# Output stage joined to the mixing stage, nine sums kept in SBUF, and token tiles of four neighbouring tokens a partition

## The reference

```python
proj = xn @ in_proj_w + in_proj_b            # 256 -> 768
v = proj[..., :256]
for i in range(2):                           # two orders
    ctrl = proj[..., (i + 1) * 256:(i + 2) * 256]
    h = implicit_filter(...)                 # one causal filter per channel, 2048 taps
    v = fft_conv(v, h)                       # causal convolution along the tokens
    xc = depthwise_conv3(ctrl) + conv_b
    v = v * xc * sigmoid(xc @ gate_w + gate_b)
mixed = v @ out_proj_w + out_proj_b
h = bitlinear(xn, w_fc) + gate * (xn @ v_ffn.T @ fast_b.T @ u.T)
ffn = bitlinear(relu(h) ** 2, w_proj)        # 256 -> 1024 -> 256, ternary weights
out = x + mixed + ffn
```

## Time and profile before

| | |
|---|---|
| median of 3 runs | 948.92 us (948.15 to 949.27) |
| the profiled execution | 947.57 us |
| its span, first to last instruction | 946.0 us |
| TensorE busy with matmuls | 842.4 us (89%) |
| TensorE busy with weight loads | 699.2 us (74%) |
| VectorE, ScalarE, GpSimd busy | 633.3, 496.6, 248.4 us |
| DMA | 151.4 MB, 160 GB/s over the span |
| mean granted TensorE clock | 0.959 |

### The profile page before, as it was taken

One profiled execution on the slowest core, in us unless ns is written; L12 is line 12 of the kernel. 1 busy time (PEld: TensorE's weight loads), 2 busy tenths in 40 slices (PEclk: granted clock), 3 DMA queues, 4 the chain that ended last, 5 costly groups with the idle time before them and its releaser, 6 DMA issues.

```text
span 946.0 us, 26422 instructions
## 1 busy us (share of the span) xinstructions
PE 842.4 (89%) x9894; PEld 699.2 (74%) x9895; DVE 633.3 (67%) x1041; ACT 496.6 (52%) x694; POOL 248.4 (26%) x267
## 2 busy tenths in 40 slices
PE   3937999999999964999999999979999999984995
PEld 1325878888888853888888888868888888873885
DVE  6953898998989973456565565556556656653885
ACT  6422877777777772344444444434445344434761
POOL 1023555646646501011121121211112111110111
PEclk9977999999999986899999999999999999995999
DMA  6363224233242138587778868766887777696897
GB/s 182 115 192 134 91 92 177 89 130 136 89 155 111 78 104 261 91 177 175 164 151 195 183 156 176 144 162 153 179 162 173 184 164 168 125 195 148 250 320 273
DMA packets 86866, 151.41 MB, mean 160 GB/s; under 512 B 13013, under 2 KB 62566, under 8 KB 85798
## 3 DMA queue, kind: packets, MB, share of 16 engines
q1 hardware_dynamic: 74918, 107.50, 47.6%
q0 software_dynamic: 11472, 41.69, 13.1%
q10 hardware_dynamic: 432, 1.64, 0.5%
HBM read 102.11 MB, written 48.69 MB: 159 GB/s over the span
## 4 chain that ended last, share of the span: by engine, by line
PE 41%; DVE 7%; DMA 6%; issue 5%; ACT 1%; POOL 0%; DVEq 0%; SPq 0%; ACTq 0%; POOLq 0%
PE pp L1112 13%; PE py L1131 12%; PE pf L1084 11%; PE pf L1090 3%; DVE xb L969 2%; DMA out<-GC 2%; PE py L1099 2%; DMA GC<-xf_hbm 2%; DVE r L974 1%; DVE pp L964 1%; DMA xf_hbm<-xb 1%; DVE r_lo L979 1%; DMA lead<-filters 1%; DMA tokens<-xnT_hbm 1%; PE po L415 1%
## 5 line engine op out<-in xcount | busy, mean ns | idle before, releaser
L1131 PEld LDWEIGHTS py<-vwin,lead 64*64 64x64 f32 x5120 | 134.6, 134 | 30.5 <-issue 30.5
L1044 ACT ACTIVATE r_hi<-r 128x512 fp32r<-128x512 f32 x128 | 80.8, 631 | 137.7 <-DVE r L974 137.7
L1131 PE MATMUL py<-vwin,lead 64*64 64x128 f32 (+4 forms) x5120 | 148.3, 267 | 5.2 <-issue 3.1
L1039 ACT ACTIVATE r<-pf,fscale 128x512 f32<-128x512 f32 x128 | 87.9, 687 | 122.5 <-PE pf L1090 120.4
L979 DVE TENSOR_TENSOR r_lo<-r,r_hi 128x512 fp32r<-128x512 f32 x128 | 103.7, 810 | 68.4 <-ACT r_hi L1044 68.4
L1112 PE MATMUL pp<-wproj,r_hi 128*128 128x256 f32 x512 | 135.7, 298 | 9.9 <-DVE r_lo L979 3.6
L1084 PE MATMUL pf<-tokens,split_a 128*128 (+1 forms) x512 | 140.2, 395 | 0.0
L1112 PE MATMUL pp<-wproj,r_lo 128*128 128x256 f32 x512 | 127.2, 282 | 0.0
L1112 PEld LDWEIGHTS pp<-wproj,r_hi 128*128 128x128 f32 x512 | 96.4, 188 | 26.8 <-issue 9.0
L456 POOL TENSOR_SCALAR lead<-lead,norms 128x256 f32<-128x256 f32 x64 | 114.1, 1794 | 3.4 <-POOL norms L450 3.4
L616 DVE SCALAR_TENSOR_TENSOR xc<-ctrl,taps,xc 128x512 f32<-128x512 f32 x128 | 97.2, 778 | 18.8 <-ACT xc L688 18.1
(11 more groups left out here) (164 smaller groups left out, 1546.4 us busy)
## 6 DMA issues: line engine op xcount, KB each, us to landing
lead<-filters SPq DMA_DIRECT2D x128, 320.0 KB, 6.0
xnT_hbm<-split_b SPq DMA_DIRECT2D x32, 512.0 KB, 3.1
tokens<-xnT_hbm POOLq DMA_DIRECT2D x32, 512.0 KB, 7.1
lead<-in_attn_x SPq DMA_DIRECT2D x16, 512.0 KB, 3.8
gc_hbm<-xc SPq DMA_DIRECT2D x16, 512.0 KB, 2.6
xb<-in_attn_x POOLq DMA_DIRECT2D x16, 512.0 KB, 7.5
GC<-gc_hbm SPq DMA_DIRECT2D x32, 256.0 KB, 7.8
GC<-xf_hbm SPq DMA_DIRECT2D x16, 512.0 KB, 7.9
```

The costliest lines, as they stand in the source:

```text
L1039: act.activation(r[j][:, :], pf[j][:, :], ACT.Relu, scale=fscale[:, m:m + 1]).then_inc(relu_done, 1)
L1044: act.activation(r_hi[j][:, :], r[j][:, :], ACT.Copy).then_inc(r_hi_done, 1)
L1131: last = pe.matmul(py[g % 2][q * BW:(q + 1) * BW, side, l, :, A:NB], tile[rows, q * PAIR + l, j * BW:(j + 1) * BW], vwin[g % 2][rows, q, l ...
```

## The change

1. **Joined.** The output stage's work stands in `mix_stage`'s block, with no barrier ahead of it. Its PSUM tiles are the mixing stage's (`pT` on `py`, `po` on `pf` and `pp`), the split `yg` lies where the ternary weights lay, and the output weights are split in the last iteration. The first two chunks' transposes are put before the last two `proj`. The copy to `ys` is gone: TensorE reads `V` itself as the stationary operand of the transposes, whose 128 columns lie 128 values apart there. The loops of the output part are written out.
2. **Nine sums kept.** The sums of chunks 7 to 15 are made and stay in `GC1`, whose first-order gates are used up by then; only chunks 0 to 6 go through `xf_hbm`. The output part begins with the kept chunks (`position`). Seven chunks' gates are loaded during the second order's iterations (`ahead`).
3. **Token tiles.** Tokens `p * 4 + i` stand at partition `p`, so that the four tokens of a partition are neighbours in HBM, for the loads of `x` in this stage and the writes of `out`. The stationary operands of `proj` and `projected` are read by a step of four to match.
4. The first two filter tiles of the mixing stage, not one, are requested at the end of `project_stage`.

```diff
+KEPT = NCH // ORDERS + 1
+FIRST_KEPT = NCH - KEPT
+GATES = NCH - KEPT
...
+        pT = [p[:, :, :, :, :].rearrange("p r l n a -> p (r l n a)").rearrange("p (t k j) -> p t k j", t=TB, k=KT) for p in py]
+        po = [pf[:, :, :].rearrange("p j (t d) -> p (j t) d", d=D), pp[:, :, :]]
+        ygs = [[half_[:, part, :].rearrange("p (k t) -> p k t", k=KT) for part in range(2)] for half_ in splits]
+        out_tiles = out.rearrange("n (q p i) d -> (n q) p i d", i=TT, p=P)
...
+            def ahead(m, g):
+                if m == 0 and g == GPI - 1:
+                    sp.wait_ge(y_out, GROUPS // ORDERS + 2)
+                if m == 2 and g == 0:
+                    sp.wait_ge(xf_saved, 16 * FIRST_KEPT)
+                    load_wo(sp, wo)
+                piece = m * KT + g // KT - 1
+                if g % KT and 0 <= piece < GATES * KT:
+                    load_gates(sp, piece // KT, (piece % KT,))
...
-            x_tiles = x.rearrange("n (q i p) d -> (n q) p i d", i=TT, p=P)
+            x_tiles = x.rearrange("n (q p i) d -> (n q) p i d", i=TT, p=P)
...
+            for p in range(NCH):
+                pool.wait_ge(out_ready, p + 3)
+                pool.dma_start(out_tiles[position(p)], sums[p % KEPT]).then_inc(out_saved[p % KEPT], 16)
...
             for order in range(ORDERS):
-                lagging(dve, order, lambda m, it, first: body(order, m, it, first))
+                lagging(dve, order, lambda m, it, first: body(order, m, it, first), True)
+            gated(0)
             low(NCH - 1, HT - 1)
+            yg_low(0)
+            gated(1)
             scale(NCH - 1)
-            add(NCH - 1)
+            add(NCH - 1, sums[KEPT - 1])
+            yg_low(1)
+            for p in range(2, NCH):
+                gated(p)
+                summed(p - 2)
+                yg_low(p)
+            for p in (NCH - 2, NCH - 1):
+                summed(p)
...
-                        last = pe.matmul(pp[:, i, :], part[m % 2][:, i * P:(i + 1) * P], wproj[:, m, :],
+                        last = pe.matmul(pp[:, i, :], part[m % 2][:, i::TT], wproj[:, m, :],
...
+            def transposed(p):
+                i, c = p % 2, position(p)
+                pe.wait_ge(yg_ready, p + 1)
                 for t in range(TB):
-                    last = pe.transpose(pT[i][:, t, :, :].rearrange("p k j -> p (k j)"), ys[i][:, t, :], ident[:, :])
+                    last = pe.transpose(pT[i][:, t, :, :].rearrange("p k j -> p (k j)"), V[:, :, c // CPB, (c % CPB) * TB + t], ident[:, :])
                 last.then_inc(yT_mm, 1)
...
+            def projected(p):
...
                 for t in range(TT):
-                    ts = slice(t * P, (t + 1) * P)
+                    ts = slice(t, CH, TT)
                     for k in range(KT):
                         last = split_mm(pe, po[i][:, t, :], (ygs[i][0][:, k, ts], ygs[i][1][:, k, ts]),
                                         (wos[0][:, k, :], wos[1][:, k, :]), k == 0, k == KT - 1)
...
+            def stages(far):
+                for order in range(ORDERS):
+                    mixed(order, far)
+                pe.wait_ge(y_out, GROUPS + 2)
+                transposed(0)
+                proj(NCH - 1, HT - 2)
+                transposed(1)
+                proj(NCH - 1, HT - 1)
+                pe.wait_ge(wo_split, 1)
+                pe.wait_ge(relu_done, NCH * HT + 2)
+                projected(0)
+                pe.wait_ge(xf_ready, NCH + 1)
+                for p in range(2, NCH):
+                    transposed(p)
+                    projected(p - 1)
+                projected(NCH - 1)
```

More of the change, by code:

```diff
@@ L896, in body @@
                             sp.sem_inc(mid_loaded[g % 2], 16 * SIDES)
+                        if order:
+                            ahead(m, g)
                         if far:
+                            if first and g == 0:
+                                sp.wait_ge(T_loaded[1], 16 * SIDES)
                             wait_alone(sp, group_mm, G + 2, sp_passed)
@@ L901, in body @@
                                 wait_alone(sp, far_used, G * FARS + (j + 1), sp_passed)
[L902 to L912 removed]
+                if order == 0:
+                    lagging(sp, order, body)
+                    return
@@ new lines, in loads @@
+                for m in range(ITERS):
+                    body(m, m + ITERS, False)
+            def ahead(m, g):
[7 more added lines that the diff above has]
+                    load_gates(sp, piece // KT, (piece % KT,))
@@ new lines, in gates @@
+            def gates(p):
+                wait_alone(sp, yg_ready, p - GATES + 3, sp_passed)
+                load_gates(sp, p)
+            def stages(far):
+                for order in range(ORDERS):
+                    loads(order, far)
+                for p in range(GATES, NCH):
+                    gates(p)
+                    if p >= KEPT:
+                        wait_alone(sp, out_saved[p - KEPT], 16, sp_passed)
+                        load_sum(sp, p - KEPT)
+            with sp.If(tail < 1):
+                stages(False)
@@ L1003, in body @@
                     if closing:
-                        add(it - 1)
+                        add(it - 1, kept_sum(m) if order else xb[:, :, :])
                     square(it, 2 * g + 1)
+                    if last and g == 1:
+                        dve.wait_ge(wo_hi_ready, 1)
+                        dve.tensor_tensor(wos[1][:, :, :], wo, wos[0][:, :, :].bitcast(F32), ALU.subtract).then_inc(wo_split, 1)
                     if g < GPI - 1:
@@ L1083, in fc @@
                     for part in range(2):
-                        last = pe.matmul(pf[m % 2][:, :], tern[:, k, ws], tokens(even, part, k), start=(k == part == 0), stop=False)
+                        last = pe.matmul(pf[:, m % 2, :], tern[:, k, ws], tokens(even, part, k), start=(k == part == 0), stop=False)
                     if k == 0 and passed is not None:
```

322 lines of the change are left out of this document (120 added, 202 removed).

## The result

The change makes the kernel slower: 1065.77 us (median of 4 runs, 1064.29 to 1070.82) against 948.53 us for the kernel before beside it (4 runs, 943.55 to 949.27), a ratio of 1.126 with a 95% interval of 1.120 to 1.131. The profiled execution took 1064.72 us, its span 1062.8 us, at a mean granted clock of 0.975.

The account below looks back on a forecast made before the run. TensorE was taken to bound the mixing stage. First output product at 850.8 + 89 + 1.8 = 941.6, then 105.4, 1.3 and 6.0 us: span 1054.3, time 1057 us, range 916 to 1075.

Parts of the forecast that it names:

- what the joining gives: Between the stages and in the output: first output product at 850.8 us, span 918.6 us, 27 us less.
- They lie beside TensorE: In the mixing stage, nine saves and nine reloads dropped from DMA traffic give no further gain.
- 3.76 us a chunk: In the output, TensorE's 8 transposes (0.79 us) and 24 pairs of weight load and product (2.97 us).
- only the transposes pay: Variant of free loads in the output: transposes cost 14 x 0.9 = 13 us more, time 934 us.
- the second early tile: At the mixing stage's start, competing with the first tokens: between nothing and about 3 us, taken as nothing.
- The step of four: Weight loads of proj and the output: a load of 0.107 us doubles, pairs go to 0.213 us; chance 0.50.
- The first half of the rule: SBUF is read in 16-byte lines, two accesses per line for full speed, each crossing pays; by it the 1057 us sum holds.
- The mixing stage: 128 proj at 0.71 us more make 91 us, less some 2 us of VectorE waits: +89 us.
- The gap: From last feed-forward product to first output product: shrinks from 19 us to some 3 us, at the higher clock level.
- Free loads: Rival on TensorE's stationary reads: the step doesn't show, time 921.5 us; chance 0.38 with the two smaller variants.
- partly slower loads: Rival on weight loads: one and a half times, 0.160 us each, 40 us in mixing, about 980 us; chance 0.12.
- VectorE as the bound: Rival in the output with free loads: chunks stay at 4.4 us, 8 us more, 930 us; within free loads' 0.38.

Follow-up runs that it names:

- both mended: The joining without the step, plus ScalarE's copy of V for chunks 2 to 15 and a later load of x for kept sums: 915.60 us, ratio 0.967.

## Why the prediction was right

**What bounds, and what the joining gives.** TensorE bounds both stages, as read. The first output product without the step starts at 850.54 us (850.8 foretold), and the joining gives 945.9 - 928.4 = 17.5 us where the working had 27. The start is luck in part: the stage's start, 4.4 us earlier, offsets the waits for filter tiles, which the working had at nothing. Two terms of that sum were mis-sized. "They lie beside TensorE" was said of the kept sums' DMA traffic: it cost 6 to 8 us, since dropping the saves took away what had spaced the loads of `x`, and the forecast priced removed transfers, not the new time of those that stay. And 3.76 us a chunk forgot that the transposes' step isn't free even if the pairs' is; the working's own case "only the transposes pay" (934 us) had it too dear, at 0.9 us a chunk against 0.3. The output took 3.9 us more than foretold (65.7 for 61.8), the end of the span 2.5. With both mended the joining gives 31.7 us, 4 us more than foretold, about what the stage's earlier start is there (371.49 us for 375.31). The mixing stage's first wait was 11.7 us and is 6.9 to 9.7 in the changed kernel and its versions: the second early tile shows no cost, and whether it is what brings the start forward wasn't tested.

**The step of four.** Taken: 0.213 us a load. Measured: 0.233, the upper bound that ScalarE's copy gave with its factor of 2.2. The forecast put the time for this factor at 1085 us and let its range end at 1075, short of it. The load came at the full factor, and the time stayed inside the range only because the transposes were cheaper and more waits vanished than the working had: that is luck too. That the row of another engine, writing by a longer step, priced this load to two digits is luck in part: a transpose with a step of 128, nearer to that row in its step, pays only 0.14. The mechanism is shown for the products. The first half of the rule that the forecast weighed (the Trainium skill, "SBUF — State Buffer", section on Door 1: lines of 16 bytes, two accesses to a line for full speed) agrees with steps of two, three and four, at 0.12, 0.175 and 0.233 us; its sentence that a stride of up to four float32 is free doesn't hold for a stationary operand.

**The mixing stage.** +89 us foretold. The first output product moved from 850.54 to 945.43, 94.9 us. By the working's own count it should be 128 x 7.5 x 0.115 = 110 us less the waits that vanish; the forecast took 2 us for those, though the earlier trace rows alone show 3.6 and 3.2 us for VectorE. Without the step TensorE waited 18.5 us in the stage behind its first wait (8.1 for filters, 3.6 for `r_lo`), and with it 5.2 (none and 1.7). That is 13 of the 15 us that lie between 110 and 94.9; the other 2 are the stage's start, 368.79 us for 370.89. Two errors of opposite sign, 19 us in the load (110 against 91) and 13 in waits and start (15 against 2), left 6.

**The output.** A chunk: 5.1 + 1.7 = 6.8 us foretold, 6.79 measured. That is again a balance: 24 pairs take 24 x 0.233 = 5.6 us, 0.5 more, and 8 transposes 1.11 us, 0.6 less. From the first product to the end of the last sum 106.7 us were foretold (105.4 and 1.3); it took from 945.43 to 1053.06, 107.6. The end of the span came 9.7 us after the last sum where 6.0 were taken from before; in the version without a step it is 8.5 us as well, and in the kernel before with the step alone 5.5, so it comes with the joining and not with the longer pieces. The last bytes of `out` move before 1056 us: from there to the end of the span it is over 6 us, where the kernel before has 2 (944 to 946). The added time lies behind the last write, and its cause stays open.

**The gap.** 3 us foretold, 0.23 measured: with slow pairs the last two `proj` cover the first chunk's gating, conversion and split. The faster versions show 0.8 us of waiting there. The clock stayed at its upper level (1.00), as foretold. In the kernel before it was at the lower level (0.50) from 855 to 871 us, and so still when TensorE began its output: the eight transposes at 867.42 took 1.97 us where 1.04 is usual. I estimate from these durations that some 2 us of the joining's gain are the clock's.

**What fell.** Free loads, partly slower loads and VectorE as the bound are excluded: VectorE waits 3.14 us a chunk. Where the loads are fast and the transposes too, VectorE does hold every second chunk, by 0.2 us, and not the 0.64 us of the rival. The sum came to 1057 against 1065.77 us; of the 9 us, 3.8 are in the start of the output (945.4 for 941.6), 0.9 in its length, 3.7 at the end.

## What to carry to other kernels

Reading a stationary operand by a step is an edit to TensorE's weight loads: count the 16-byte stretches that 128 values touch, and compare the load with the product that is to hide it. A step of two was hidden under 256 columns and a step of four was not; when neighbours in a partition are wanted, let ScalarE's read of PSUM take the step, which left the relu at 687 ns here. And when a save or any spacing transfer is removed, look at what now goes out right behind another transfer: one wait that put a load in the middle of an iteration gave 6 to 8 of the 31.7 us.

## What the runs showed of the hardware

- A stationary load of 128 columns of float32: 0.111 us contiguous, hidden at 0.118 by a step of two, 0.175 by three, 0.233 by four, 0.242 by eight, 0.224 by sixteen. Contiguous and by four it is the same in plain float32 (0.112 and 0.233 a pass), and by four the same beside products of 256, 128 and 64 columns.
- A moving operand by a step of four: 0.92 ns a column, 0.235 us for 256, where contiguous ones take no more than 0.118.
- A transpose's load doesn't follow this: 0.11 us by steps of 2 to 32, 0.14 by 64 and 128. The cause is open.
- ScalarE reads PSUM by a step of four at no cost (687 ns for 512 elements either way). Its copy in SBUF that reads short runs and writes by a step of 128 takes 2057 ns where a conversion of as many neighbouring elements takes 1061; which side of it pays wasn't tested.
- With a 512 KB load issued right behind the tokens, two filter tiles of 320 KB took 8.9 and 11.9 us to land, where the median is 6.0 and the slowest of the kernel before 9.3, and TensorE waited 6.4 to 9.5 us for such tiles in five versions; with the load later it waited 3.2 and 1.2.
